# First sweep of an adjacency kernel: split operands, remainders on two engines, held tiles loaded late

## The reference

```
inv_deg = 1.0 / (jnp.sum(adj, axis=1) + beta)                  # layer 0
x = _layernorm(x + inv_deg[:, None] * (adj @ x + beta[:, None] * x) @ kernel + bias)

h = relu(adj @ (x @ W1) + b1)                                  # layer 1, 20 columns
h = relu(adj @ (h @ W2) + b2)                                  # 20 columns
h = relu(adj @ (h @ W3) + b3)
x = _layernorm(x + relu(h + x))

d_inv_sqrt = 1.0 / (jnp.sqrt(jnp.sum(adj, axis=1)) + 1e-8)     # layer 2
x = _layernorm(x + (adj * d_inv_sqrt[:, None] * d_inv_sqrt[None, :]) @ (x @ W + b))

B = softmax((x @ W_l) @ (x @ W_r).T) @ x                       # layer 3
x = _layernorm(x + adj @ x + gamma * (B @ W_h @ W_g))
```

## Time and profile before

| | |
|---|---|
| median of 3 runs | 1341.96 us (1341.93 to 1343.07) |
| the profiled execution | 1341.3 us, its span 1339.5 us |
| TensorE busy | 1285.0 us (96%) |
| VectorE busy | 930.6 us (69%) |
| ScalarE busy | 715.7 us (53%) |
| GpSimd busy | 267.5 us (20%) |
| HBM read | 284.98 MB |

### The profile page before, as it was taken

One profiled execution on the slowest core, in us unless ns is written; L12 is line 12 of the kernel. 1 busy time (PEld: TensorE's weight loads), 2 busy tenths in 40 slices (PEclk: granted clock), 3 DMA queues, 4 the chain that ended last, 5 costly groups with the idle time before them and its releaser, 6 DMA issues.

```text
span 1339.5 us, 17278 instructions
## 1 busy us (share of the span) xinstructions
PE 1285.0 (96%) x5911; PEld 792.2 (59%) x5911; DVE 930.6 (69%) x1207; ACT 715.7 (53%) x880; POOL 267.5 (20%) x175
## 2 busy tenths in 40 slices
PE   8999999999999899999999999998899999999987
PEld 3544444433232233778787788886677767767764
DVE  6666665551010365999999989896888788788885
ACT  1111111011110123688787877776788788788795
POOL 0111110010000010011111100005234334354345
PEclk9999999998999999999999999999999999999999
DMA  9886665555999899899999999970000000000000
GB/s 367 314 316 251 251 219 204 173 188 181 382 333 400 309 352 407 307 353 374 351 371 359 376 356 361 382 291 0 1 0 1 1 1 1 1 18 14 1 1 32
DMA packets 81087, 288.01 MB, mean 215 GB/s; under 512 B 9466, under 2 KB 11130, under 8 KB 81018
## 3 DMA queue, kind: packets, MB, share of 16 engines
q1 hardware_dynamic: 78768, 286.30, 57.2%
...
HBM read 284.98 MB, written 2.10 MB: 214 GB/s over the span
## 4 chain that ended last, share of the span: by engine, by line
PE 79%; DVE 8%; ACT 4%; issue 4%; DMA 3%; POOL 1%; POOLq 0%; ACTq 0%; DVEq 0%; SPq 0%
PE acc L1298 17%; PE acc L1536 7%; PE acc L1454 7%; PE acc L1388 7%; PE acc L1449 6%; PE acc L1450 6%; DMA raw<-in_adj_s 3%; DVE t_lo L1029 2%; PE rs L1306 2%; PE acc L1526 2%; PE acc L1527 2%; PE acc L1530 2%; PE e L1491 2%; PE e L1493 2%; PE rs L1491 2%
## 5 line engine op out<-in xcount | busy, mean ns | idle before, releaser
L1029 DVE TENSOR_TENSOR t_lo<-raw,t_hi 128x1024 fp32r<-128x1024 f32 x256 | 311.1, 1259 | 26.7 <-ACT t_hi L743 21.8
L743 ACT ACTIVATE t_hi<-raw 128x1024 fp32r<-128x1024 f32 x256 | 261.5, 1054 | 40.5 <-PE acc L1454 39.9
L1449 PE MATMUL acc<-t_hi,st_hi 128*128 128x512 f32 x512 | 201.9, 394 | 0.9 <-ACT t_hi L743 0.9
L1450 PE MATMUL acc<-t_hi,st_lo 128*128 128x512 f32 x512 | 199.5, 390 | 0.0
L613 POOL TENSOR_TENSOR ring_lo<-ring,p_hi 128x1024 fp32r<-128x1024 f32 x64 | 155.4, 2429 | 220.0 <-ACT p_hi L799 219.9
L1298 PE MATMUL acc<-raw,x 128*128 128x512 f32 x400 | 179.3, 597 | 0.0
L1454 PE MATMUL acc<-t_lo,st_hi 128*128 128x512 f32 x512 | 159.5, 393 | 5.8 <-DVE t_lo L1029 5.0
L1103 DVE TENSOR_TENSOR ring<-ring,e 128x1024 f32<-128x1024 f32 x128 | 154.0, 1212 | 0.1
L793 ACT ACTIVATE ring<-ring 128x1024 f32<-128x1024 f32 x128 | 134.2, 1054 | 25.0 <-DVE ring L1103 24.9
L1298 PEld LDWEIGHTS acc<-raw,x 128*128 128x128 f32 x400 | 73.7, 190 | 92.0 <-issue 92.0
L1536 PE MATMUL acc<-ring,x 128*128 128x512 f32 x256 | 120.2, 592 | 0.0
...
## 6 DMA issues: line engine op xcount, KB each, us to landing
...
```

The lines of the kernel that those rows point to most:

```text
L743: nc.scalar.activation(t_hi[:, g % HL, :], raw[:, k, :], ACT.Copy).then_inc(hi_done, 1)
L1029: nc.vector.tensor_tensor(t_lo[:, k, :], raw[:, slot_no(s, c, g), :], t_hi[:, k, :].bitcast(F32), ALU.subtract).then_inc(lo_done, 1)
L1449: mm(a[:, :], block_of(st_h, b), hi[:, m], start=(g == 0 and j == 0), stop=False)
L1450: mm(a[:, :], block_of(st_l, b), hi[:, m], start=False, stop=False)
```

## The change

Sweep 0 takes the form of the wide sweeps. x is loaded in place of x0, ScalarE rounds it to x_hi and VectorE makes x_lo. ScalarE rounds each half tile into t0_hi (four slots, a new buffer), and the remainder t_lo is made by VectorE or, for the n in POOL_LO of the row, by GpSimd: 58 of 128. TensorE does six single pass products a half tile, the eight with t0_hi of two half tiles first (`leading`), then those with t_lo. The fused products stay float32. h_a gets a 21st column of ones, so that fused tiles add their own row sums in the bank `ahead`; VectorE's `row_sum` runs only over the plain half tiles (PLAIN), and TensorE adds the fused part with `row_picker`.

The new buffers take the place of held tiles, so rows 0 to 3 (LATE) are all streamed in sweep 0, and their 16 held half tiles are loaded when it has ended, row 3 first. FILL moves to held rows 4 and 5. Counts of half tiles streamed: 112 in sweep 0 (100 before), 150 after it (150 before).

```
-LATE = 1
-FILL = {0: (0, 1), 2: (2, 3)}
+LATE = (0, 1, 2, 3)
+FILL = {4: (4, 5), 5: (5,)}
...
-        mine = {1: [6, 7, 5], 2: [1, 0, 3, 2]}[s]
+        mine = {1: [6, 7], 2: [1, 0, 3, 2]}[s]
...
+PLAIN = [[n for n, i in enumerate(ITEMS[0, c]) if not i.fused] for c in range(NC)]
+POOL_LO = ((1, 2, 4, 6, 7, 9, 11, 12, 14), (0, 2, 3, 5, 7, 8, 10, 12, 13, 15), (0, 2, 4, 6, 8, 10, 11, 13, 15),
+           (0, 2, 4, 6, 8, 10, 12, 14), (0, 2, 4, 6, 8, 10, 12, 14), (0, 3, 6, 9, 12, 15), (1, 5, 9, 13), (1, 5, 9, 13))
...
+        with ExitStack() as early:
+            t0_hi = sb("t0_hi", [P, HL, TW], F32R, early)
...
+                x_hi = sb("x_hi", [P, NB * D], F32R, early)
...
-                x0 = sb("x0", [P, NB * D], F32, early)
+                x_lo = sb("x_lo", [P, NB * D], F32R, early)
```

SP, the late tiles:

```
             def load_late():
                 sp.wait_ge(pe_acc, NC)
-                for d in KEPT[LATE]:
-                    for h in range(2):
-                        sp.dma_start(kept_tile(LATE, d, h), tile(LATE, 2 * d + h)).then_inc(late_in, 16)
+                for c in reversed(LATE):
+                    for d in KEPT[c]:
+                        for h in range(2):
+                            sp.dma_start(kept_tile(c, d, h), tile(c, 2 * d + h)).then_inc(late_in[c], 16)
```

GpSimd:

```
+            def remainder(c, n):
+
+                u = c * NG + n
+                pool.wait_ge(hi_done, u + 1)
+                nc.gpsimd.tensor_tensor(t_lo[:, u % HL, :], tile_of(0, c, ITEMS[0, c][n]),
+                                        t0_hi[:, u % HL, :].bitcast(F32), ALU.subtract).then_inc(lo_pool_done, 1)
+
+            def first_row(c):
+                for n in range(NG):
+                    if n == 1 and c > 0:
...
+                        keep_old_x(0, c - 1)
+                    if n == 5:
+                        if c > 0:
+                            pool.wait_ge(pe_acc, c)
+                            alone(pool)
+                        nc.gpsimd.tensor_tensor(blocks(bx[:, :]), blocks(cols(x, c)), spread(cols(beta, c, CB)),
+                                                ALU.mult).then_inc(S["bx"], 1)
+                    if n == 13 and c > 0:
+                        pool.wait_ge(S["norm"], done("norm", 0, c - 1))
+                        alone(pool)
+                        nc.gpsimd.tensor_copy(cols(x, c - 1), xn[:, :]).then_inc(S["xw"], 1)
+                    if n in POOL_LO[c]:
+                        remainder(c, n)
```

ScalarE, in `first_row` for each n (the parts of the epilogue of row c - 1 follow at n = 2, 4, 8, 10 and 12, `next_h` at the end):

```
+                    if c == 0 and n % (NG // XP) == 0:
+                        operand_hi(n * XP // NG)
+                    wait_tile(act, 0, c, i)
+                    if u >= HL:
+                        act.wait_ge(pe_tile, SPLIT_AT[divmod(u - HL, NG)])
+                    nc.scalar.activation(t0_hi[:, u % HL, :], tile_of(0, c, i), ACT.Copy).then_inc(hi_done, 1)
```

VectorE:

```
+            def first_row(c):
+                for n in range(NG):
+                    if c == 0 and n % (NG // XP) == 0:
+                        operand_lo(n * XP // NG)
+                    if n not in POOL_LO[c]:
+                        remainder(c, n)
+                    if n in PLAIN[c][1:]:
+                        row_sum(c, PLAIN[c].index(n))
+                    if n == PLAIN[c][-1]:
+                        fold(c)
+                    if c > 0:
+                        if n == 4:
+                            residual_1(0, c - 1)
...
+                        if n == 8:
+                            scales(0, c - 1)
```

TensorE:

```
+                def leading(n):
+                    i, hi = items[n], t0_hi[:, n % HL, :]
...
+                    pe.wait_ge(hi_done, c * NG + n + 1)
+                    for j in range(GB):
+                        b, m = i.d * CB + i.h * GB + j, slice(j * CW, (j + 1) * CW)
+                        mm(a[:, :], block_of(x_hi, b), hi[:, m], start=(n == 0 and j == 0), stop=False)
+                        mm(a[:, :], block_of(x_lo, b), hi[:, m], start=False, stop=False)
+
                 for n, i in enumerate(items):
...
+                    if n % 2 == 0:
+                        leading(n)
+                        leading(n + 1)
+                    lo = t_lo[:, n % HL, :]
+                    wait_lo(pe, c, n)
                     for j in range(GB):
...
+                        b, m = i.d * CB + i.h * GB + j, slice(j * CW, (j + 1) * CW)
+                        k = mm(a[:, :], block_of(x_hi, b), lo[:, m], start=False, stop=False)
+                    k.then_inc(pe_tile, 1)
```

More of the change, by code:

```diff
@@ L19 @@
 H = 20
+HA = H + 1
 NB = N // P
@@ L88, in held @@
 def held(s, c, d):
-    return d in KEPT[c] and not (s == 0 and c == LATE)
+    return d in KEPT[c] and not (s == 0 and c in LATE)
 def order_of(s, c):
@@ L125, with first_counts, sums_through, lo_through @@
 ITEMS, T_WIDE = plan()
+PLAIN = [[n for n, i in enumerate(ITEMS[0, c]) if not i.fused] for c in range(NC)]
+POOL_LO = ((1, 2, 4, 6, 7, 9, 11, 12, 14), (0, 2, 3, 5, 7, 8, 10, 12, 13, 15), (0, 2, 4, 6, 8, 10, 11, 13, 15),
+           (0, 2, 4, 6, 8, 10, 12, 14), (0, 2, 4, 6, 8, 10, 12, 14), (0, 3, 6, 9, 12, 15), (1, 5, 9, 13), (1, 5, 9, 13))
+def first_counts():
+    split, joint, at = {}, {}, 0
+    for c in range(NC):
+        for n, i in enumerate(ITEMS[0, c]):
+            at += 1
+            split[c, n] = at
+            if i.fused and i.h == 1:
+                at += 1
+                joint[c, n - 1] = joint[c, n] = at
+    return split, joint, at
+SPLIT_AT, JOINT_AT, BASE_0 = first_counts()
+T_FIRST = sum(not i.kept for c in range(NC) for i in ITEMS[0, c])
+def sums_through(c, n):
+    return sum(len(PLAIN[q]) - 1 for q in range(c)) + max(PLAIN[c].index(n), 1)
+def lo_through(c, n):
+    by_pool = n in POOL_LO[c]
+    return by_pool, sum((m in POOL_LO[q]) == by_pool for q in range(c + 1) for m in range(NG) if (q, m) <= (c, n))
+DVE_LO = sum(m not in POOL_LO[c] for c in range(NC) for m in range(NG))
 STORES = [(s, r) for s in FLAT for r in range(NC) if any(i.fused for i in ITEMS[s, r])]
@@ L242, in build @@
         h_b = rsum[:, 0:NB * H]
+        row_folded = sums[:, 0, :]
+        row_picker = comb[:, H:HA]
         w_t = bx
@@ L349, in wait_ring, with wait_lo @@
                 return
-            for r in range(NC):
-                for n, i in enumerate(ITEMS[0, r]):
+            for c in range(NC):
+                for n, i in enumerate(ITEMS[0, c]):
                     if i.seq == t:
-                        sp.wait_ge(sum_done, r * NSUM + max(n, 1))
-            sp.wait_ge(pe_tile, t + 1)
+                        wait_lo(sp, c, n)
+                        if i.fused:
+                            sp.wait_ge(pe_tile, JOINT_AT[c, n])
+                        else:
+                            sp.wait_ge(sum_done, sums_through(c, n))
+                        return
+            sp.wait_ge(pe_tile, ring_through(t))
+        def wait_lo(eng, c, n):
+            by_pool, count = lo_through(c, n)
+            eng.wait_ge(lo_pool_done if by_pool else lo_done, count)
         def wait_row(eng, s, r):
             if s > 0 and not ITEMS[s, r][-1].kept:
-                eng.wait_ge(pe_tile, ITEMS[s, r][-1].seq + 1)
+                eng.wait_ge(pe_tile, ring_through(ITEMS[s, r][-1].seq))
             else:
@@ L563, in stationary5_lo @@
                                         ALU.subtract).then_inc(st5_lo_done, 1)
+            def remainder(c, n):
[6 more added lines that the diff above has]
+                    if n == 1 and c > 0:
+                        if c == 1:
+                            for part in range(1, XP):
+                                pool.wait_ge(x_in[part], 16)
+                        keep_old_x(0, c - 1)
[11 more added lines that the diff above has]
+                        remainder(c, n)
             def step(s, c, par):
-                has_before = not (s == 0 and first(c))
+                if s == 0:
+                    first_row(c)
+                    return
                 ps, pc = before(s, c)
@@ L571, in step @@
                     stationary5_lo(NC - 2)
-                if has_before and ps in STAGES["xb"]:
+                if ps in STAGES["xb"]:
                     keep_old_x(ps, pc)
-                if s == 0:
-                    if not first(c):
-                        pool.wait_ge(pe_acc, c)
-                        alone(pool)
-                    nc.gpsimd.tensor_tensor(blocks(bx[:, :]), blocks(cols(x, c)), spread(cols(beta, c, CB)),
-                                            ALU.mult).then_inc(S["bx"], 1)
-                if has_before and ps in STAGES["xw"]:
+                if ps in STAGES["xw"]:
                     pool.wait_ge(S["norm"], done("norm", ps, pc))
@@ L998, in flat @@
                     scales(ps, pr)
-                    dve.wait_ge(fill_mm, 1)
-                    nc.vector.tensor_copy(sums[:, 0, :], ahead[0]).then_inc(fill_done, 1)
-                    dve.wait_ge(fill_mm, 2)
-                    dve.wait_ge(sums_done, stored(0, 2))
```

(6 more changed lines are left out.)

187 lines of the change are left out of this document (108 added, 79 removed).

## The result

The changed kernel took 1422.71 us (median of 4 runs, 1419.48 to 1426.09) against 1341.95 (4 runs, 1339.07 to 1343.07): a ratio of 1.061, 95% interval 1.058 to 1.064. The prediction, 1400 with a range of 1365 to 1432, had the direction, the cause and the range right, and was 23 us low. The profiled execution took 1426.09 us, the slowest of the four.

What follows compares the result with a forecast made beforehand. An SBUF read path shared by VectorE and GpSimd bounds the first sweep's first five or six rows, TensorE the rest: 1341.3 + 57 (first sweep) + 2 (narrow sweeps) = 1400 us, range 1365 to 1432.

Steps and rivals of the forecast that it cites:

- TensorE's part: First sweep: six single pass products a half tile; rows 1 to 7 need 28.0 to 35.0 us, ending near 252 alone.
- a sign: What would show the forecast right in the first sweep: among others, rows 6 and 7 about 35 us each.
- The shared path: First sweep: VectorE and GpSimd exclude each other reading SBUF, so their times add; the path outlasts TensorE in rows 0 to 5.
- The forecast's prices: Path time in the first sweep: 2.27 us a GpSimd remainder, 1.15 a 128x1024 VectorE instruction.
- The step that failed in size: Rows 1 to 5 of the first sweep: 48.5, 45.0, 41.7, 41 and 38 us, set mainly by path time.
- Row 0: First row of the first sweep: 52.0 us of path time after a start of about 9.
- 7 of 10: Rows 4 to 7: taking the longer per part gives 10 us more, of which 7 was taken.
- The clock: TensorE's clock falls while it waits in the first sweep's early rows: 2 us taken, 0 and 40 as ends.
- Narrow sweeps: After the first sweep: 12 additional late transfers fit a DMA pause; +2 us, bounds -2 and +16.
- Two: Rival: in the first sweep the engines run side by side and it gets faster, 1312 us; chance 0.09.
- Three: Rival: the clock falls and stays low in the waiting rows, 1430 us and above; chance 0.08.
- Four: Rival: GpSimd's hold of the path is 1.3 us rather than 2.27, giving 1350 to 1367; chance 0.06.

Runs made afterwards that it cites:

- after: The changed kernel itself, against the kernel before: 1422.71 us, ratio 1.061.
- the last experiment: Changed kernel with rows 0 to 3 in float32 as before, all remainders on VectorE, one row 4 tile's row sum on TensorE: 1330.59 us, 0.993.
- the small program: Separate program, no layers: 12 VectorE additions and 6 GpSimd subtractions, alone and together; VectorE's twelve took 13.71 us alone, 26.57 together.
- the two filled kernels: Changed kernel with additional products ahead of t_lo waits, eight a pair in rows 0 to 2 or six in rows 1 to 5: 1419.15 and 1427.6 us.

## Why the prediction was right, and where it was short

**TensorE's part.** Right in the late rows. Row 7, which TensorE fills, took 36.7 in after and 35.2 to 35.3 in seven of the experiments; the forecast's need was 35.0. Row 6 took 39.7 where 35 was named as a sign. Rows 5 to 7 of the last experiment took 34.6, 34.4 and 35.2 for 32.7, 33.8 and 35.0, so row 5 was counted up to 1.9 short.

**The shared path.** Right, and shown four ways: the small program (2.14 for a GpSimd instruction, 1.14 for one of VectorE's), the stretched instructions of the changed kernel, and the two kernels that take work off the path (-60 by moving remainders to the busier engine, -86 without row sums). The forecast's prices, 2.27 and 1.15, were good, the first 0.13 high.

**The step that failed in size: that the path is always busy in rows 1 to 5.** The forecast took a row's time to be its path time there. Rows 1 to 5 took 55.8 + 51.3 + 48.7 + 42.7 + 41.5 = 240.0 where it had 214.2: 25.8 more. Laying VectorE's instructions with two operands in SBUF and all of GpSimd's on one line, from the timelines of both engines, they cover 53.7, 44.4, 42.2, 37.4 and 35.0 of these rows, 212.6 together; the counts gave 209.4. So 3.2 of the miss is path time counted too low (row 1 alone 5.2, rows 2 and 4 less than counted), and 27.4 is time in which neither engine was on the path; for that the forecast had 4.8, in rows 4 and 5. 3.2 + 27.4 - 4.8 = 25.8. The rest of the miss of the sweep's end, 348 against 374.8, is small: row 0 was 3.8 shorter, rows 6 and 7 together 2.5 longer than their 37 each, the last products take 1.1, and the forecast's sum was 1.2 under its own rows (it took 7 of 10 and added 2 for the clock). That the range held the time owes something to luck: the forecast's room above 1400 was given for the clock (up to 40) and the late tiles (up to 16), and what filled it was mostly neither.

**What made the path idle.** The timelines of rows 1 to 5 divide the 27.4. At four turns of rows the path is idle for 3.1, 3.1, 5.5 and 2.7 us, 14.5 together, and each time the next instruction on it is the t_lo whose t_hi stood in ScalarE's queue behind `at` and `sums`, 4.5, 4.4, 4.3 and 3.1 us after its slot was free. About 7.5 is VectorE's own work off the path (degrees, statistics and small scalar steps: in row 1 83.88 to 85.29 above, with GpSimd idle). The 5 or so left are mostly other waiting for t_hi. Over all five rows, t_hi were held some 73 us behind the epilogue with their slots free; most of this went by while the path was busy. So the forecast overlooked ScalarE, which is at most half busy in every row: what it holds up isn't its work but its order. The lowered clock has a part in this, since it stretches the products that `at` waits for: the last fused ones and the closing ones took 3.4 us before the `at` above (211.1 to 214.5), and 2.2 at the sweep's end (372.7 to 374.8). Behind it all two queues that each run in order share a path that doesn't know which instruction is urgent, so a remainder for a later half tile goes first, as in the turn of row 1. It isn't the pairs (1425.0 without them). All this is read from timelines and not tried: no kernel was run with the epilogue placed elsewhere in ScalarE's queue, or with more t_hi slots. So the idle time and where it lies are measured, and what either change would give back is open.

**Row 0.** 57.2 against 61: the path was covered for 50.8 (52.0 in the forecast) and idle for 6.4, where I had put 9 for the start; the first x_lo began at 6.0 and the first remainder at 7.6. Rows 0 and 1 together took 113.0 against 109.5.

**The clock.** It did fall, to a mean of 0.77 to 0.96 between its levels of 1.2 and 2.4 GHz, in all eight rows; TensorE was 56 to 93% busy in rows 0 to 6. Its price was near: 2 in the forecast, 4 to 6 by the two filled kernels, with the doubts named there. It also ate what the split saves in busy time: TensorE was busy 285.3 us in the sweep, 283.4 before, and 257.8 without the row sums, where the clock stayed at 0.95 or above.

**Narrow sweeps.** +2 in the forecast, +1.2 in the trace, and 1339.44 for the late tiles alone: nothing that can be measured.

**The rivals.** Two (side by side, 1312) falls by the small program. Three (1430 and above, by a clock that stays low) is near in time, but its mechanism gave back 4 to 6 us here, not 30. Four (a shorter hold, 1350 to 1367) falls by 2.14 a GpSimd instruction where it needs 1.3.
